# An eight-block transformer kernel on one core: row sums kept in PSUM, the last additions on VectorE, logits ahead of the row scales, and the output stored in four parts

## The chip, the cores and the metric

The kernel runs on one core of one Trainium2 chip. The metric is the device time of one execution in microseconds (us), as a median over runs. The profile shows one execution. Its engines are TensorE (PE, with its weight loads as PEld), VectorE (DVE), ScalarE (ACT), GpSimd (POOL) and SyncE (SP), which here only issues DMAs.

## The reference, cut to what matters

x is 4 batches of 512 rows of 256 numbers (float32). Eight blocks are added to it in turn; the change touches the two that are called `_L1_ffn_ref`, the sixth and the eighth.

```python
x = x + mla(_layernorm(x)); x = x + ffn(_layernorm(x)); x = x + cosine(_layernorm(x)); x = x + ffn(_layernorm(x))
x = x + gated_linear_attention(_layernorm(x))
x = x + _L1_ffn_ref(_layernorm(x), ...)      # stage wsa
x = x + lora_attention(_layernorm(x))
x = x + _L1_ffn_ref(_layernorm(x), ...)      # stage wsb
return x

def _L1_ffn_ref(x, workspace, ...):          # S = 16 slots, K = 4, NB = 2 rounds, 4 heads
    for _ in range(NB):
        logits = _rms(x, norm_pre_w) @ compete_w.T + compete_b
        vals, idx = top_k(swapaxes(logits, 1, 2), K)          # 4 rows of 512 for each slot
        written = softmax(vals)-weighted sum of the chosen rows of (x @ write_w.T + write_b)
        ws = _rms(ws + written, norm_post_w)
        att = softmax of (x @ wq.T + bq) against (ws @ wk.T + bk), over the 16 slots, 4 heads
        x_b = att applied to (ws @ wv.T + bv), @ out_proj_w.T + out_proj_b
        x = _rms(x + x_b, norm_post_w)
    return x
```

## The kernel before

The kernel is a row of stages. Each is one function with a block in which every engine runs its own hand-written list of instructions, held together by semaphores. After each stage `Kit.clear_sems` (L48 to L54) opens a block of its own in which POOL clears that stage's semaphores one by one; all engines meet at the start and at the end of each block. Nothing reorders the lists: what stands first in the code of an engine runs first.

`x` stays in SBUF for the whole program, as 16 tiles of 128 rows (4 for each batch). `workspace_ffn` runs twice, as stage `wsa` and, after `lora_attention`, as stage `wsb`. It works on `xf`, a normalised copy of x. At the start of a round PE turns the tiles of `xf` (`turn`, L1927) into two PSUM banks for each batch (`WS_TURN_BANKS`), ACT (round 0) or DVE (round 1) copies them out as `xfT`. Then:

- `spread_scales` (PE, L1937) puts the 16 columns of row scales `inv[:, 0, :]`, which POOL has computed (L1832), as rows into bank 4; it waits for the scales of batch 3 and for `xfT` of batch 1. ACT copies bank 4 to `rows` (L1888).
- `bid` (PE, L1947) multiplies `xfT` with the compete weights into bank 0: the logits. It waits for `xfT` of batch 3.
- `choose` (DVE, from L1692) waits for both, multiplies the logits by `rows`, and picks the four best rows. PE, DVE, ACT and POOL then hand the work to each other (`select`, `write`, `scores`, softmax, `read`) down to `read` (PE, L2040), which leaves the stage's x_b in the PSUM banks of each batch.
- `add_read(r, b)` (DVE, L1769) writes x_b + `xf` to `xsum`, an SBUF buffer for two batches; so it drains DVE before it uses a half again (batches 2 and 3).
- `mean_squares(1, b, ...)` (ACT, L1874) takes four squares with sums from `xsum`, `row_scales(1, b)` (POOL, L1830 and L1832) makes `inv[:, 1, :]` of them, and `norm_sum(r, b)` (DVE, L1778) writes the scaled rows to `xf`.

DVE's order at the end of a round is add 0, add 1, norm 0, add 2, norm 1, add 3, norm 2, norm 3. After round 1 POOL adds `xf` to `x`, one instruction of 128x1024 for each batch (L1862), and it does so after all of its row scales. After stage `wsb` and its clearing, `store_output` opens one more block, in which SP stores all of x with one DMA of 2 MB and waits for it (L2771).

## Time and profile before

| | us |
|---|---|
| median of 3 runs (2426.75 to 2430.74) | 2427.96 |
| the profiled execution, its own time | 2429.51 |
| span of the profiled execution, first to last instruction | 2427.7 |
| stage wsa, about | 1762 to 1911 |
| stage wsb, about | 2268 to 2416 |
| PE busy over the span | 2008.8 (83%) |
| DVE, ACT, POOL busy over the span | 1067.3, 801.7, 529.6 |

A busy share is an average over stages: in the two stages that the change touches PE is busy less than half of the time. Times in the rows below are us from the span's start. A row's bracket is the time for which the engine stood idle before it, and what ended that. PEclk is the granted clock of TensorE, 1.00 for 2.4 GHz and 0.50 for 1.2 GHz.

### The profile page before, as it was taken

To read this page: it belongs to the slowest core of one execution; us is meant where nothing else is said; L and a number is where in the kernel's file an instruction comes from. 1 tells how busy PE (TensorE), PEld (TensorE's weight loads), DVE (VectorE), ACT (ScalarE), POOL (GpSimd) and SP (SyncE) were. 2 spreads that over 40 slices of the span, in tenths; PEclk is the share of its full clock that TensorE was granted. 3 is DMA by queue.
4 is the path that set the end of the run, shared out by engine and by line. 5 is a ranking of instruction groups with operands and counts; after the bars stand their busy time and mean duration, and the time that the engine had idled before them with its cause. 6 is when DMAs were issued, how large, how long until landed. Compare 5 with 4: busy or idle time off the path is not lost. (4 is left out here: it accounts for less than half of the span.)

```text
span 2427.7 us, 28846 instructions
## 1 busy us (share of the span) xinstructions
PE 2008.8 (83%) x10760; PEld 1264.3 (52%) x10760; DVE 1067.3 (44%) x2279; ACT 801.7 (33%) x1749; POOL 529.6 (22%) x618
## 2 busy tenths in 40 slices
PE   7999999995799999999999994788755288889553
PEld 4565565654467766766666682333333144444332
DVE  4545545453223333332433223388555644445454
ACT  2544434451233233323323311411113134445132
POOL 2322323220101111011110000055311533342212
PEclk9999999997799999999999996999866689999666
DMA  6000000000000000000000001000000000000001
GB/s 239 1 1 1 1 1 1 1 1 30 1 1 1 1 1 1 1 1 1 1 1 1 1 1 63 0 0 0 0 1 1 1 1 1 1 1 1 1 1 35
DMA packets 9715, 23.87 MB, mean 10 GB/s; under 512 B 2400, under 2 KB 6256, under 8 KB 8816
## 3 DMA queue, kind: packets, MB, share of 16 engines
q1 hardware_dynamic: 8288, 18.92, 2.1%
q10 hardware_dynamic: 1296, 3.18, 0.4%
q8 instruction: 85, 1.39, 0.2%
q14 instruction: 46, 0.38, 0.1%
HBM read 20.00 MB, written 2.10 MB: 9 GB/s over the span
## 5 line engine op out<-in xcount | busy, mean ns | idle before, releaser
L1221 PEld LDWEIGHTS cos_ps<-cos_vx,cos_probs 128*128 128x128 f32 x2048 | 238.4, 191 | 33.6 <-issue 28.7
L1221 PE MATMUL cos_ps<-cos_vx,cos_probs 128*128 128x129 f32 x2048 | 239.5, 274 | 4.2 <-DVE cos_on L918 4.2
L1212 PE MATMUL cos_ps<-cos_qT,cos_kT 128*128 128x512 f32 x512 | 231.3, 596 | 1.4 <-ACT cos_qT L1074 1.4
L1103 ACT ACTIVATE cos_probs<-cos_ps 128x512 f32<-128x512 f32 x256 | 151.0, 598 | 161.9 <-PE cos_ps L1212 160.8
L366 ACT ACTIVATE probs<-sc,nmax 128x512 f32<-128x512 f32 (+3 forms) x256 | 132.6, 525 | 191.0 <-DVE nmax L229 189.0
L473 PE MATMUL sc<-kT,qT 128*128 128x512 f32 (+3 forms) x512 | 173.6, 461 | 4.3 <-DVE probsT L241 2.5
L1018 POOL TENSOR_TENSOR cos_qrs<-cos_qse,neg_half 128x4 f32<-128x4 f32 x64 | 64.5, 1008 | 511.2 <-DVE cos_qse L900 511.2
L2346 DVE TENSOR_REDUCE cos_wq<-lora_ps 128x2 f32<-128x1024 f32 (+3 forms) x128 | 101.9, 824 | 104.2 <-PE lora_ps L2589 103.2
L1212 PEld LDWEIGHTS cos_ps<-cos_qT,cos_kT 128*128 128x128 f32 x512 | 94.7, 192 | 97.4 <-issue 94.1
L898 DVE TENSOR_REDUCE cos_qss<-cos_qsq 128x4 f32<-128x512 f32 x64 | 43.9, 686 | 209.1 <-ACT cos_qsq L1082 209.1
L446 PE MATMUL pq<-xnT,wap 128*128 128x512 f32 x256 | 129.0, 628 | 3.1 <-DVE swp L221 3.1
L229 DVE TENSOR_REDUCE nmax<-sc 128x1 f32<-128x512 f32 (+3 forms) x256 | 112.5, 484 | 34.5 <-PE sc L475 31.7
L1200 PE MATMUL cos_ps<-cos_wq,cos_xnT 128*128 128x512 f32 x256 | 124.5, 610 | 0.0
L1241 PE MATMUL cos_ps<-cos_wout,cos_onT 128*128 128x256 f32 x512 | 115.7, 379 | 0.0
L2577 PE MATMUL lora_ps<-lora_kT,lora_qT 32*128 32x256 f32 (+3 forms) x512 | 103.8, 481 | 10.9 <-DVE lora_wvo L2324 2.7
L473 PEld LDWEIGHTS sc<-kT,qT 128*128 128x128 f32 x512 | 81.0, 193 | 60.6 <-issue 59.0
L1074 ACT ACTIVATE cos_qT<-cos_ps 128x512 f32<-128x512 f32 x64 | 38.2, 597 | 224.1 <-PE cos_ps L1191 224.1
L1426 POOL TENSOR_TENSOR gla_qs<-cos_wout,gla_q_now 128x512 f32<-128x512 f32 x64 | 84.8, 1324 | 113.5 <-DVE cos_wout L1380 110.2
L2464 ACT ACTIVATE lora_probsT<-lora_ps 128x768 f32<-128x768 f32 (+1 forms) x96 | 84.6, 882 | 61.9 <-PE lora_ps L2582 60.9
L2582 PE MATMUL lora_ps<-lora_qT,lora_kT 32*128 32x256 f32 (+3 forms) x512 | 102.5, 483 | 1.8 <-ACT lora_probsT L2464 1.1
L1241 PEld LDWEIGHTS cos_ps<-cos_wout,cos_onT 128*128 128x128 f32 x512 | 95.1, 190 | 13.3 <-issue 1.6
L2407 POOL TENSOR_SCALAR_AFFINE_SELECT lora_probsT<-lora_probsT 128x256 f32<-128x256 f32 x128 | 50.3, 410 | 204.0 <-ACT lora_probsT L2464 202.5
(462 smaller groups left out, 3503.0 us busy)
## 6 DMA issues: line engine op xcount, KB each, us to landing
onT<-in_mla_wqT SPq DMA_DIRECT2D x1, 2048.0 KB, 9.1
mla_wo<-in_mla_wo SPq DMA_DIRECT2D x1, 2048.0 KB, 19.4
cos_wq<-in_cos_wq SPq DMA_DIRECT2D x1, 2048.0 KB, 25.5
cos_wout<-in_cos_wout SPq DMA_DIRECT2D x1, 2048.0 KB, 29.9
out<-x SPq DMA_DIRECT2D x1, 2048.0 KB, 7.5
x<-in_x SPq DMA_DIRECT2D x1, 1536.0 KB, 14.6
wq_pe<-in_mla_wq_pe ACTq DMA_DIRECT2D x1, 1024.0 KB, 14.2
x<-in_x SPq DMA_DIRECT2D x1, 512.0 KB, 4.2
```

Of the source, the lines that this page charges most:

```text
L229: red = dve.tensor_reduce(nmax[:, j, qi:qi + 1], sc[:, j, at:at + (qi + 1) * P], AX.X, ALU.max, negate=True)
L366: ex = act.activation(probs[:, j, at:at + (qi + 1) * P], sc[:, j, at:at + (qi + 1) * P], ACT.Exp, bias=nmax[:, j, qi:qi + 1], accum_out=ls ...
L446: last = pe.matmul(pq[:, :], wap[:, c, p, kind, :], xnT[:, b % 2, c, :], start=(c == 0), stop=(c == DC - 1))
L473: pe.matmul(sc[:, j, at:at + (qi + 1) * P], qT[:, n % 2, j, qi * P:(qi + 1) * P], kT[:, b % 2, j, 0:(qi + 1) * P], start=True, stop=False)
L1103: act.activation(probs[:, n % 2, kj, :], ps[:, kj, :], ACT.Exp).then_inc(s["e_done"], 1)
L1200: last = pe.matmul(ps[:, banks["project", b, u], :], xnT[:, b % 2, c, i * P:(i + 1) * P], wq[:, c, 512 * hq:512 * (hq + 1)], start=(c == 0 ...
L1212: pe.matmul(ps[:, kj, :], kT[:, b % 2, kj * P:(kj + 1) * P], qT[:, hq % 2, h % 4, :], start=True, stop=True).then_inc(s["s_ready"], 1)
L1221: last = pe.matmul(po[:, qi // 2, qi % 2, :], probs[:, n % 2, kj, qi * P:(qi + 1) * P], vx[:, b % 2, kj, :], start=(kj == 0), stop=(kj == ...
L1241: last = pe.matmul(y[i], onT[:, n % 2, a, :], wout[:, 8 * half + a, :], start=(half == 0 and a == 0), stop=(half == 1 and a == 7))
L2346: last = dve.tensor_reduce(qs[:, batch % 2, qi, h:h + 2, LORA_HD], ps[:, at:at + 2, col:col + n], AX.X, ALU.max, negate=True)
L2577: pe.matmul(ps[:, at + j, col:col + w], qT[r:r + LORA_SLOT, qi * P:(qi + 1) * P], kT[r:r + LORA_SLOT, n % 2, 0:w], start=True, stop=False)
L2582: turned = pe.matmul(ps[:, at + 2 + j, col:col + w], kT[r:r + LORA_SLOT, t % 2, kj * P:(kj + 1) * P], qT2[r:r + LORA_SLOT, kj * P:], start ...
```

## The change

Both calls of `workspace_ffn`:

- `add_read` writes its sum back into the PSUM banks it reads; `xsum` is gone, and so is the drain for batches 2 and 3. ACT's squares and `norm_sum` read PSUM (`read_tile`).
- `norm_sum` of round 1 writes its product into PSUM too, drains, and adds it to `x` on DVE in two instructions of 128x512. POOL's four additions are gone.
- PE issues `bid` before `spread_scales`.

In stage `wsb` only: SP waits in the stage's own block for each batch of x and stores it with a DMA of 512 KB; the stage's block ends when all four have landed, and the clearing comes after that. `store_output` and its block are gone. Each stage has two semaphores more to clear, 52 for 50.

```diff
+            @block.sync
+            def _(sp):
+                if out is None:
+                    return
+                for b in range(B):
+                    sp.wait_ge(s["x_ready"], b + 1)
+                    sp.dma_start(out[b, :, :].rearrange("(i p) d -> p i d", p=P), x[:, tiles(b), :])\
+                      .then_inc(s["stored"], 16)
+                sp.wait_ge(s["stored"], 16 * B)
...
                     dve.wait_ge(s["xb_ready"], 2 * r + b // 2 + 1)
-                    if b >= 2:
-                        dve.drain()
                     for h in range(2):
                         at = b * TI + 2 * h
-                        last = dve.tensor_tensor(xsum[:, b % 2, 2 * h:2 * h + 2, :],
-                                                 bank(read_bank(b, h)).rearrange("p (i d) -> p i d", i=2),
-                                                 xf[:, at:at + 2, :], ALU.add)
+                        both = bank(read_bank(b, h)).rearrange("p (i d) -> p i d", i=2)
+                        last = dve.tensor_tensor(both, both, xf[:, at:at + 2, :], ALU.add)
...
-                        last = dve.scalar_tensor_tensor(xf[:, n, :], xsum[:, b % 2, i, :], inv[:, 1, n:n + 1],
+                        rows_out = xf[:, n, :] if r + 1 < WS_NB else read_tile(b, i)
+                        last = dve.scalar_tensor_tensor(rows_out, read_tile(b, i), inv[:, 1, n:n + 1],
                                                         g["ws_post"][:, :], ALU.mult, ALU.mult)
-                    last.then_inc(s["xf_ready"], 1)
+                    if r + 1 < WS_NB:
+                        last.then_inc(s["xf_ready"], 1)
+                        return
+                    dve.drain()
+                    for h in range(2):
+                        at = b * TI + 2 * h
+                        last = dve.tensor_tensor(x[:, at:at + 2, :],
+                                                 bank(read_bank(b, h)).rearrange("p (i d) -> p i d", i=2),
+                                                 x[:, at:at + 2, :], ALU.add)
+                    last.then_inc(s["x_ready"], 1)
...
-                for b in range(B):
-                    pool.wait_ge(s["xf_ready"], WS_NB * B + b + 1)
-                    pool.tensor_tensor(x[:, tiles(b), :], xf[:, tiles(b), :], x[:, tiles(b), :], ALU.add)
...
-                        mean_squares(1, b, [xsum[:, b % 2, i, :] for i in range(TI)]).then_inc(s["m2_ready"], 1)
+                        mean_squares(1, b, [read_tile(b, i) for i in range(TI)]).then_inc(s["m2_ready"], 1)
...
+                    bid(r)
                     spread_scales(r)
-                    bid(r)
```

On DVE at the end of stage `wsb` (round 1) the list of before is, from `add_read` of batches 0 and 1 on (line numbers are those of each kernel; `wsb_ps` is PSUM):

```order
L1769 TENSOR_TENSOR wsb_xsum<-wsb_ps,wsb_xf 128x512 x4
L1778 SCALAR_TENSOR_TENSOR wsb_xf<-wsb_xsum,wsb_inv,ws_post 128x256 x4
L1769 TENSOR_TENSOR wsb_xsum<-wsb_ps,wsb_xf 128x512 x2
L1778 SCALAR_TENSOR_TENSOR wsb_xf<-wsb_xsum,wsb_inv,ws_post 128x256 x4
L1769 TENSOR_TENSOR wsb_xsum<-wsb_ps,wsb_xf 128x512 x2
L1778 SCALAR_TENSOR_TENSOR wsb_xf<-wsb_xsum,wsb_inv,ws_post 128x256 x8
```

and after it:

```order
L1780 TENSOR_TENSOR wsb_ps<-wsb_ps,wsb_xf 128x512 x4
L1788 SCALAR_TENSOR_TENSOR wsb_ps<-wsb_ps,wsb_inv,ws_post 128x256 x4
L1796 TENSOR_TENSOR x<-wsb_ps,x 128x512 x2
L1780 TENSOR_TENSOR wsb_ps<-wsb_ps,wsb_xf 128x512 x2
L1788 SCALAR_TENSOR_TENSOR wsb_ps<-wsb_ps,wsb_inv,ws_post 128x256 x4
L1796 TENSOR_TENSOR x<-wsb_ps,x 128x512 x2
L1780 TENSOR_TENSOR wsb_ps<-wsb_ps,wsb_xf 128x512 x2
L1788 SCALAR_TENSOR_TENSOR wsb_ps<-wsb_ps,wsb_inv,ws_post 128x256 x4
L1796 TENSOR_TENSOR x<-wsb_ps,x 128x512 x2
L1788 SCALAR_TENSOR_TENSOR wsb_ps<-wsb_ps,wsb_inv,ws_post 128x256 x4
L1796 TENSOR_TENSOR x<-wsb_ps,x 128x512 x2
```

The two additions to x of batches 0, 1 and 2 stand ahead of the next batch's work on the same engine; those of batch 3 are the last.

At the very end, POOL before (the `ISA` rows are the clearing of semaphores):

```order
L1832 TENSOR_TENSOR wsb_inv<-wsb_mse,neg_half 128x4
L1862 TENSOR_TENSOR x<-wsb_xf,x 128x1024 x4
L1665 UNCONDITIONAL_BRANCH
L51 UNCONDITIONAL_BRANCH
L54 ISA x50
L50 UNCONDITIONAL_BRANCH
```

and POOL after:

```order
L1851 TENSOR_TENSOR wsb_inv<-wsb_mse,neg_half 128x4
L1667 UNCONDITIONAL_BRANCH
L51 UNCONDITIONAL_BRANCH
L54 ISA x52
L50 UNCONDITIONAL_BRANCH
```

The additions have left POOL, and the DMAs, which stood behind the clearing, now stand ahead of it (on SP, `L1674 DMA out<-x 128x4x256 x4`).

On PE at the head of a round the rows of before and, below them, those of after:

```order
L1927 MATMUL wsb_ps<-ident,wsb_xf 128x128 x32
L1937 MATMUL wsb_ps<-ident,wsb_inv 32x128 x16
L1947 MATMUL wsb_ps<-wsb_xfT,wsb_cw 32x512 x8
L1954 MATMUL wsb_ps<-ident,wsb_selw 128x128 x4
```

```order
L1943 MATMUL wsb_ps<-ident,wsb_xf 128x128 x32
L1963 MATMUL wsb_ps<-wsb_xfT,wsb_cw 32x512 x8
L1953 MATMUL wsb_ps<-ident,wsb_inv 32x128 x16
L1970 MATMUL wsb_ps<-ident,wsb_selw 128x128 x4
```

The logits (`wsb_cw`) and the row scales (`wsb_inv`) have changed places; this holds in both rounds of both stages. ACT's copy of the spread scales, which DVE waits for, so comes behind both.

## Rows read from the trace of the kernel before

**Rows 1.** The page, its first part: busy us, share of the span, instructions.

```profile
PE 2008.8 (83%) x10760; PEld 1264.3 (52%) x10760; DVE 1067.3 (44%) x2279; ACT 801.7 (33%) x1749; POOL 529.6 (22%) x618
```

**Rows 2.** Timeline (start us, us, what) of DVE, stage wsb, end of round 1.

```profile
2395.97 1.68 DVE L1778 SCALAR_TENSOR_TENSOR wsb_xf<-wsb_xsum,wsb_inv,ws_post 128x256 f32<-128x256 f32 x4 [2.19 <-POOL wsb_inv L1832]
2397.74 1.29 DVE L1769 TENSOR_TENSOR wsb_xsum<-wsb_ps,wsb_xf 128x512 f32<-128x512 f32 x2
...
2400.70 1.29 DVE L1769 TENSOR_TENSOR wsb_xsum<-wsb_ps,wsb_xf 128x512 f32<-128x512 f32 x2
...
2405.38 7.93 DVE L1778 SCALAR_TENSOR_TENSOR wsb_xf<-wsb_xsum,wsb_inv,ws_post 128x256 f32<-128x256 f32 x4 [1.30 <-POOL wsb_inv L1832]
```

**Rows 3.** Timeline of POOL, the same stretch.

```profile
2404.33 1.01 POOL L1832 TENSOR_TENSOR wsb_inv<-wsb_mse,neg_half 128x4 f32<-128x4 f32 x1
2405.50 7.52 POOL L1862 TENSOR_TENSOR x<-wsb_xf,x 128x1024 f32<-128x1024 f32 x3 [0.16 <-issue]
2413.38 2.34 POOL L1862 TENSOR_TENSOR x<-wsb_xf,x 128x1024 f32<-128x1024 f32 x1 [0.36 <-DVE wsb_xf L1778]
```

**Rows 4.** Timeline, end of stage wsa (POOL) and start of the next stage (DVE).

```profile
1908.48 2.35 POOL L1862 TENSOR_TENSOR x<-wsa_xf,x 128x1024 f32<-128x1024 f32 x1 [0.36 <-DVE wsa_xf L1778]
1914.95 1.41 DVE L61 BATCH_NORM_STATS2 lora_stats<-x 128x6 f32<-128x256 f32 x4 [6.55 <-PEq L50]
```

**Rows 5.** Timeline of DVE, start of stage wsa.

```profile
1761.90 1.41 DVE L61 BATCH_NORM_STATS2 wsa_stats<-x 128x6 f32<-128x256 f32 x4 [2.81 <-PEq L50]
```

**Rows 6.** Timeline of SP: the issue of the output's DMA.

```profile
2419.81 0.40 SPq L2771 DMA_DIRECT2D out<-x  x1
```

**Rows 7.** The page, DMA issues: KB each, us from issue to landing.

```profile
out<-x SPq DMA_DIRECT2D x1, 2048.0 KB, 7.5
...
x<-in_x SPq DMA_DIRECT2D x1, 512.0 KB, 4.2
```

**Rows 8.** Windows: stretch, us, busy us (count) by engine, PEclk, DMA share, GB/s.

```profile
2422.00:2423.00 1.00, 0.00 (x0) 0.00 (x0) 0.00 (x0) 0.00 (x0) 0.00 (x0) 0.50 1.03 345
```

**Rows 9.** Timeline of ACT, DVE and PE, stage wsb, head of round 0.

```profile
2285.24 1.09 ACT L1869 ACTIVATE wsb_xfT<-wsb_ps 128x512 f32<-128x512 f32 x2 [0.62 <-PE wsb_ps L1927]
2286.64 0.60 ACT L1888 ACTIVATE wsb_rows<-wsb_ps 128x512 f32<-128x512 f32 x1 [0.31 <-PE wsb_ps L1937]
...
2288.45 0.69 DVE L1692 TENSOR_TENSOR wsb_lraw<-wsb_ps,wsb_rows 128x512 f32<-128x512 f32 x1 [4.22 <-PE wsb_ps L1947]
...
2281.53 3.67 PE L1927 MATMUL wsb_ps<-ident,wsb_xf 128*128 128x128 f32 x16 [2.00 <-DVE wsb_xf L1675]
```

**Rows 10.** Timeline of DVE, stage wsb, head of round 1.

```profile
2342.29 4.88 DVE L1686 COPY wsb_xfT<-wsb_ps 128x512 f32<-128x512 f32 x8
2353.58 0.69 DVE L1692 TENSOR_TENSOR wsb_lraw<-wsb_ps,wsb_rows 128x512 f32<-128x512 f32 x1 [6.41 <-PE wsb_ps L1947]
```

**Rows 11.** Windows: wsb, L1937 and L1947 of round 0, L1937 of round 1, two turns.

```profile
2285.49:2286.47 0.98, 0.98 (x33) 0.84 (x34) 0.00 (x0) 0.83 (x2) 0.00 (x0) 1.00 0.00 0
2286.47:2288.39 1.92, 1.92 (x20) 0.46 (x16) 0.00 (x0) 0.60 (x1) 0.00 (x0) 1.00 0.04 9
2348.40:2350.11 1.71, 1.71 (x33) 1.58 (x36) 0.00 (x0) 0.00 (x0) 0.00 (x0) 0.50 0.00 0
2339.38:2344.28 4.90, 3.87 (x16) 3.10 (x16) 3.66 (x8) 4.54 (x21) 3.60 (x5) 0.50 0.00 2
```

**Rows 12.** Windows: stage wsa, L1947 of round 1.

```profile
1844.42:1848.06 3.64, 3.64 (x23) 0.59 (x12) 0.00 (x0) 0.60 (x1) 0.00 (x0) 0.51 0.00 0
```

**Rows 13.** Groups by line and shape: out<-in xcount, busy us, mean ns, idle before.

```profile
L1376 DVE TENSOR_TENSOR gla_ps<-gla_ps,gla_kT 128x512 f32<-128x512 f32 x64 | 43.4, 678 | 4.6 <-ACT gla_decay L1458 3.2 <-PE gla_ps L1522 1.4
L1720 DVE TENSOR_TENSOR wsb_wsum<-wsb_ps,wsb_wsb 128x256 f32<-128x256 f32 x2 | 0.9, 426 | 2.4 <-PE wsb_ps L1971 2.4
L1797 DVE TENSOR_TENSOR wsb_wsb<-ws_start,ws_write_b 128x256 f32<-128x256 f32 x1 | 0.4, 420 | 0.0
L1913 ACT ACTIVATE wsb_ash<-wsb_ash 128x512 f32<-128x512 f32 x4 | 2.5, 630 | 4.2 <-DVE wsb_ash L1750 4.2
```

More of the change, by code:

```diff
@@ L1594, with workspace_ffn @@
 WS_TURN_BANKS = ((0, 2), (4, 6), (1, 3), (5, 7))
-def workspace_ffn(nc, g, tag):
+def workspace_ffn(nc, g, tag, out=None):
     with ExitStack() as ctx:
@@ L1610, in workspace_ffn @@
         xf = sb("xf", [P, NT, D])
-        xsum = sb("xsum", [P, 2, TI, D])
         xfT = sb("xfT", [P, DC, NT * P])
@@ L1651, in workspace_ffn @@
                  "a_ready", "a_copied", "at_ready", "ash_ready", "ae_ready", "att_ready", "pt_ready", "attT_ready",
-                 "xb_ready", "xsum_ready", "m2_ready", "r2_ready")
+                 "xb_ready", "xsum_ready", "m2_ready", "r2_ready", "x_ready", "stored")
         s = {n: k.sem(f"{tag}_{n}") for n in names}
@@ L1663, in read_bank, with read_tile @@
             return WS_TURN_BANKS[b][half]
+        def read_tile(b, i):
+            return bank(read_bank(b, i // 2))[:, (i % 2) * D:(i % 2 + 1) * D]
         with nc.Block() as block:
+            @block.sync
[7 more added lines that the diff above has]
+                sp.wait_ge(s["stored"], 16 * B)
             @block.vector
@@ L2756, in build @@
         lora_attention(nc, g)
-        workspace_ffn(nc, g, "wsb")
-        store_output(nc, g, out)
-def store_output(nc, g, out):
-    with ExitStack() as ctx:
-        stored = Kit(nc, ctx).sem("stored")
-        with nc.Block() as block:
-            @block.sync
-            def _(sp):
-                sp.dma_start(out.rearrange("b (i p) d -> p (b i) d", p=P), g["x"][:, :, :]).then_inc(stored, 16)
-                sp.wait_ge(stored, 16)
+        workspace_ffn(nc, g, "wsb", out)
 def kernel(**inputs):
```

## The prediction

> **What bounds the kernel now.** Read first the page's busy shares: PE 83% [rows 1]. That would make every edit off PE worthless, and it is an average. So the next view is the timeline of the two stages that change, wsa and wsb, and there the idle times in the brackets: at each step one engine waits for another, and no engine is the bound. What counts is the chain of handovers. Three places of it matter.
>
> The end of a stage. At 2405.34 POOL has the last row scales (2404.33 + 1.01) [rows 3]; from then on only DVE's last `norm_sum` and the four additions to x are left. DVE's takes 7.93 us where the same four instructions took 1.68 three batches earlier [rows 2]. Beside them POOL runs three additions in 7.52 us, and the fourth, 2.34, after DVE [rows 3]. The two engines hold each other up. The stage's work ends at 2413.38 + 2.34 = 2415.72.
>
> The end of the program. From 2415.72 to the DMA's issue at 2419.81 [rows 6] there are 4.09 us in which POOL clears 50 semaphores and the engines meet; the DMA lands 7.5 us later [rows 7], at 2427.3, and the span ends at 2427.7.
>
> The head of a round. DVE waits for `bid` (L1947), 4.22 us in round 0 [rows 9] and 6.41 in round 1 [rows 10]. `spread_scales` runs ahead of it, and ACT's copy of the scales (0.60) lies beside `bid` [rows 9].
>
> **Part 1: additions on DVE.** Walk through round 1 of wsb from 2395.97 [rows 2]. I use: four products 1.67, two sums 1.29, 0.09 for a drain (2397.65 to 2397.74), and an instruction that doesn't wait starts 0.08 before the end of the one ahead. Norm 0 ends at 2397.65, its new additions run 2397.74 to 2399.03, add 2 ends at 2400.24, norm 1 at 2401.83, its additions at 2403.2, add 3 at 2404.41 (before: 2400.70 + 1.29 = 2401.99), norm 2 with its additions at 2407.4. The scales of batch 3 came 3.35 after add 3 (2405.34 - 2401.99), so now at 2407.76: DVE has been free for 0.4. Norm 3 and its drain and additions take 1.67 + 0.09 + 1.29: x is complete at 2410.85, and 2415.72 - 2410.85 = **4.9 us** are gained. In wsa the stage's last addition ends at 1908.48 + 2.35 = 1910.83 [rows 4], with the same distances, so **4.9 us** again. These additions were not free on POOL; on DVE, 2.4 of their 5.2 us delay add 3, and that is in the walk.
>
> **Part 2: sums in place in PSUM.** DVE's sum: 128x512 in place in PSUM took 678 ns in another stage [rows 13], against 0.69 for such an operation with its output in SBUF [rows 9]: nothing. DVE's product with PSUM on one or both sides is not in the trace. Nearest: an addition of 128x256 with one input in PSUM 426 ns, with both in SBUF 420 [rows 13]. I take 0, bounds -0.02 and +0.07 for each. Some 12 products are on the chain of a round, 48 in all: -1.0 to +3.4 us. A rule speaks against this: the Trainium skill ("VectorE: DVE Perf Modes", The TRN2 errata) gives a VectorE operation 58 cycles over its elements from SBUF and 120 from PSUM, which would be an estimate of 65 ns more for each product, or 3.1 us over the 48. The trace's 426 against 420 disagrees with it, so the sum goes without.
>
> ACT's squares read PSUM. A 128x512 pass took 0.60 from PSUM [rows 9] and 630 ns from SBUF, with another function [rows 13]; so -0.03 each, eight on the chain of a round, 32 in all: -1.0, bounds -1.5 and 0. I take half, **-0.5**.
>
> The drain ahead of add 2 and add 3: without it the sum starts 0.08 before the product's end instead of 0.09 behind it, 0.17 each. Both feed the chain to the scales of batch 3 in round 0: 4 x 0.17 = **-0.7**. In round 1 the walk has it.
>
> **Part 3: logits first.** Round 0 of wsb: `xfT` of batch 3 is there at 2286.33 (2285.24 + 1.09) [rows 9], `bid` started at 2286.47, so it gains 0.1. Then 0.98 of `spread_scales` [rows 11], which lay in PE's idle time, stands behind `bid`, and behind it ACT's copy with its handovers, 0.7, which lay beside `bid`: DVE starts at 2286.4 + 1.92 + 0.98 + 0.7 = 2290.0 for 2288.45, **+1.6**. That is with the clock at 1.00. Before the change it rose while PE went from the turns into `spread_scales` with at most 0.3 of idle time; now there is a pause of 1.2 us between the last turn (2281.53 + 3.67 = 2285.20 [rows 9]) and `bid`. In round 1 two turns with a pause of 1.0 between them stayed at 0.50 to their end [rows 11]. At 0.50 `bid` takes 3.64 and `spread_scales` 1.71 [rows 11, 12], so the head would take 1.7 + 0.7 more: **+4.0**. When the clock rises differs from run to run, and was in this execution already up for both; I take +2.3 for the mix (bounds 1.6 and 4.0).
>
> Beside that the Trainium skill ("TensorE: Matmul & The Clock Gate", Part 1) says that the gate's observation runs free of the kernel, so that the place where the clock rises shifts from run to run. The trace is one run and shows one place.
>
> Round 1 of wsb: the copies end at 2342.29 + 4.88 = 2347.17 [rows 10], the scales only at about 2348.4 [rows 11]. `bid` (3.64) ends at 2350.8, `spread_scales` (1.71) at 2352.5, less some 0.3 for a clock that rises on the way, the copy at 2352.9: DVE starts 0.6 ahead of 2353.58, **-0.6**. wsa is alike: its heads hold the same rows. For two stages: 2 x (2.3 - 0.6) = **+3.4**, bounds +2.0 and +6.8.
>
> **Part 4: the output.** Three of the four DMAs are issued from 2399.0, 2403.2 and 2407.4 and are done before the last. That one moves 512 KB. 2 MB took 7.5; at the 345 GB/s of its middle [rows 8] 1.5 MB are 4.6 us, so 2.9 are left; the 512 KB load at the program's start took 4.2 [rows 7]. I take 3.4. Nothing is queued behind SP's waits but the four DMAs. The 4.09 of meeting and clearing come after the landing now, with two more semaphores: the 32 semaphores of the stage ahead of wsa took 2.81 (the bracket of the first instruction of wsa) [rows 5], 50 took 4.12 (1910.83 to 1914.95) [rows 4], so 0.07 each and 0.15 for two. Before: 4.09 + 7.5 + 0.4 = 12.0 from the last addition to the span's end; now 3.4 + 4.1 + 0.15 + 0.1 = 7.75, **-4.2** (-4.7 to -3.4). The clearing moved, it did not go. wsa clears two more as well: **+0.15**.
>
> **The sum.** -4.9 - 4.9 - 0.5 - 0.7 + 3.4 - 4.2 + 0.15 = -11.65 against the profiled 2429.51, so 2417.9. The profiled execution stands 1.55 above the median of 2427.96; against that, **2416.3**.
>
> **Rivals.**
> 1. The clock doesn't rise in round 0. For: the pause of 1.2, and the turns at 0.50 across a pause of 1.0. Against: later stretches that began cold do rise. All four heads cold and late: +6.8 instead of +3.4, so 2419.7.
> 2. The last DMA's time hardly depends on its size (7.5 for 512 KB also). Against: the 4.2 row. It gives back 4.1: 2420.4.
> 3. The new products cost more with PSUM (0.07 each, 3.4 in all), by the skill's rule named above nearly the same. 2419.7.
> 4. The clearing at the very end isn't part of the measured time, since nothing waits for it. For: no row shows an execution that ends with one. Against: the program isn't over. 2412.2.
> 5. Slower than before: DVE and ACT, both in PSUM now at the end of each round, hold each other up as DVE and POOL did. The chain has 48 products, so it decides from 11.65 / 48 = 0.24 us on each; at a contention of 1.0 each (DVE beside POOL lost 7.93 - 1.67 = 6.3 on four) the time would be 2416.3 + 48 = 2464. Against: the in-place sums in PSUM at 678 ns ran with ACT at work there.
> 6. That the output isn't stored early: x's last batch is late anyway, so only the size of the last DMA counts. That is rival 2's price.
>
> **How the numbers follow.** Forecast 0.52, rival 1 0.20, rivals 2 and 6 0.07, rival 3 0.09, rival 4 0.08, rival 5 0.04. The range from 2411.5 to 2421.0 takes in all but the last and the sum of two bad cases. This kernel's measurement can tell 0.2%, 4.9 us: faster means below 2423.1. Faster 0.93, same 0.04, slower 0.03.
>
> **What would show it.** DVE's last `norm_sum` back at 1.7 us with the additions right behind it, and 4.9 us less from the first add of a last round to the end of the stage's work. `spread_scales` and the copy on the way from `bid` to DVE; PEclk over `bid` in round 0. The last output DMA 3 to 4 us, then some 4 us of clearing. Products near 480 ns. It is wrong if the products or squares in PSUM come out longer, if the span ends with the landing, or if the heads of round 0 cost over 4 each.

## The result, and the profile after

The changed kernel takes 2420.80 us as a median of 8 runs (2419.21 to 2423.56), the kernel before beside it 2427.43 (8 runs, 2425.68 to 2430.74). The ratio is 0.9972, with a 95% interval of 0.9961 to 0.9982: 6.6 us faster, between 4.4 and 9.5. The forecast was 11.65 us less, 2416.3. Direction and range held, the range by 0.2 us (its upper end is 2421.0); a little over half of the gain came. The measured time of an execution is 1.8 us longer than its span, before and after.

The profiled execution of the changed kernel has a span of 2421.8 us, against 2427.7, so 5.9 less. It is cut below at the same places in both. "Head" is from the start of a stage (round 0) or of the copies of `xfT` (round 1) to the product of the logits with `rows`; "choice" from there to the sum that takes the written slots; "attention" from there to the first `add_read`; "end" from there to the next round's copies, or to the last addition to x; "behind it" to the next stage or to the end of the span.

| us | before | after | difference |
|---|---|---|---|
| the three stages ahead of wsa | 1761.9 | 1762.6 | +0.7 |
| head, round 0: wsa, wsb | 20.20, 20.26 | 23.19, 21.77 | +3.0, +1.5 |
| head, round 1 | 11.53, 11.29 | 10.18, 10.26 | -1.35, -1.0 |
| choice, round 0 | 13.18, 12.99 | 14.24, 14.23 | +1.1, +1.2 |
| choice, round 1 | 13.00, 13.04 | 14.24, 14.54 | +1.2, +1.5 |
| attention, four rounds | 100.4 | 101.3 | +0.8 |
| end, round 0 | 15.84, 15.84 | 15.16, 15.16 | -0.7, -0.7 |
| end, round 1 | 24.44, 24.42 | 19.18, 19.20 | -5.3, -5.2 |
| behind wsa, behind wsb | 4.12, 11.98 | 4.31, 7.28 | +0.2, -4.7 |
| lora_attention, which nothing touches | 353.2 | 355.0 | +1.8 |

The end of the stages came as walked through. This is the timeline of DVE in stage wsb, end of round 1, of the changed kernel (start us, us, what; the bracket is idle time before, and what ended it):

```profile
2395.32 2.49 DVE L1780 TENSOR_TENSOR wsb_ps<-wsb_ps,wsb_xf 128x512 f32<-128x512 f32 x4 [4.60 <-PE wsb_ps L2056]
2399.88 1.67 DVE L1788 SCALAR_TENSOR_TENSOR wsb_ps<-wsb_ps,wsb_inv,ws_post 128x256 f32<-128x256 f32 x4 [2.06 <-POOL wsb_inv L1851]
2401.62 1.29 DVE L1796 TENSOR_TENSOR x<-wsb_ps,x 128x512 f32<-128x512 f32 x2
...
2409.89 1.29 DVE L1796 TENSOR_TENSOR x<-wsb_ps,x 128x512 f32<-128x512 f32 x2
2411.49 1.67 DVE L1788 SCALAR_TENSOR_TENSOR wsb_ps<-wsb_ps,wsb_inv,ws_post 128x256 f32<-128x256 f32 x4 [0.32 <-POOL wsb_inv L1851]
2413.23 1.29 DVE L1796 TENSOR_TENSOR x<-wsb_ps,x 128x512 f32<-128x512 f32 x2
```

The last product takes 1.67 us where it took 7.93 [rows 2], it waits 0.32 for its scales (forecast 0.4), and x is complete 1.3 us after it. The products with PSUM on both sides cost what they cost from SBUF.

SP's timeline and the page's DMA issues (KB each, us from issue to landing) show the output, and the page's clock line its lower places (tenths of full speed in 40 slices):

```profile
2402.94 11.98 SPq L1674 DMA_DIRECT2D out<-x  x4
```

```profile
out<-x SPq DMA_DIRECT2D x4, 512.0 KB, 2.9
```

```profile
PEclk9999999998799999999999997999866689999666
```

Four stores of 512 KB land 2.9 us after their issue, where the one of 2 MB took 7.5 [rows 7]. The three sixes in the middle lie over stage wsa, the last three over wsb: there the clock is low for most of the time. The kernel before has the same six sixes on its page. The timeline of PE, stage wsa, round 0, from the logits to the written slots, first of the kernel before, then of the changed one:

```profile
1778.83 1.47 PE L1937 MATMUL wsa_ps<-ident,wsa_inv 128*32 128x128 f32 x32
1780.13 1.89 PE L1947 MATMUL wsa_ps<-wsa_xfT,wsa_cw 128*32 128x512 f32 x16
1786.87 1.12 PE L1954 MATMUL wsa_ps<-ident,wsa_selw 128*128 128x128 f32 x4 [4.85 <-DVE wsa_selw L1706]
1788.77 3.64 PE L1959 MATMUL wsa_ps<-wsa_xf,wsa_selT 128*32 128x256 f32 x32 [0.78 <-DVE wsa_selT L1709]
1793.02 0.57 PE L1965 MATMUL wsa_ps<-ident,wsa_xsel 128*128 128x128 f32 x2 [0.61 <-DVE wsa_xsel L1711]
1794.11 1.13 PE L1971 MATMUL wsa_ps<-ws_write,wsa_xselT 128*128 128x256 f32 x4 [0.52 <-DVE wsa_xselT L1713]
```

```profile
1780.70 3.44 PE L1963 MATMUL wsa_ps<-wsa_xfT,wsa_cw 128*32 128x512 f32 x16 [1.27 <-ACT wsa_xfT L1885]
1783.96 1.06 PE L1953 MATMUL wsa_ps<-ident,wsa_inv 128*32 128x128 f32 x32
1790.56 1.11 PE L1970 MATMUL wsa_ps<-ident,wsa_selw 128*128 128x128 f32 x4 [5.54 <-DVE wsa_selw L1718]
1792.46 3.64 PE L1975 MATMUL wsa_ps<-wsa_xf,wsa_selT 128*32 128x256 f32 x32 [0.78 <-DVE wsa_selT L1721]
1796.71 0.69 PE L1981 MATMUL wsa_ps<-ident,wsa_xsel 128*128 128x128 f32 x2 [0.61 <-DVE wsa_xsel L1723]
1797.92 2.08 PE L1987 MATMUL wsa_ps<-ws_write,wsa_xselT 128*128 128x256 f32 x4 [0.52 <-DVE wsa_xselT L1725]
```

Two things are to be seen. The first: with the logits first, `bid` waits 1.27 us for the copies, the pause that the prediction named, and takes 3.44 us for 1.89. In stage wsb of the same execution the same pause stands ahead of `bid`, and `bid` has the high clock (the rows of before for this place are [rows 9], which are of wsb though their heading says wsa):

```profile
2287.09 1.92 PE L1963 MATMUL wsb_ps<-wsb_xfT,wsb_cw 128*32 128x512 f32 x16 [1.27 <-ACT wsb_xfT L1885]
```

So the pause alone doesn't settle which clock `bid` gets. The second: behind the choice the four matmuls that write the slots take 2.08 us for 1.13, and the two before them 0.69 for 0.57: that is the 1.06 us of the choice, at the same waits between the engines from there on. The windows of the changed kernel (stretch, us, busy us and count by engine, PEclk, DMA share, GB/s) give the clock of `bid`, of `spread_scales`, and of the stretch from the choice on:

```profile
1780.70:1784.14 3.44, 3.44 (x24) 1.06 (x28) 0.00 (x0) 0.00 (x0) 0.00 (x0) 0.55 0.00 0
1783.96:1785.02 1.06, 1.06 (x36) 0.79 (x28) 0.00 (x0) 0.00 (x0) 0.00 (x0) 1.00 0.00 0
1790.56:1803.50 12.94, 8.21 (x44) 3.85 (x44) 2.76 (x7) 0.51 (x2) 1.47 (x3) 0.50 0.01 2
```

`bid` runs almost wholly at 1.2 GHz (0.55), the clock rises at its end, `spread_scales` has 2.4 GHz (1.00), PE stands idle for 5.54 us while DVE chooses, and all that follows has 1.2 GHz again (0.50).

### The profile page after: what moved, and what is told of

The parts are those of the page before. It is cut to its first block and busy times, and to the rows that moved or that the text cites. A ratio compares the mean times of both kernels' runs of the same rounds, so it can differ in the third digit from the quotient of the medians.

```text
span 2421.8 us, 28850 instructions
## 1 busy us (share of the span) xinstructions
PE 2018.0 (83%) x10760; PEld 1271.6 (53%) x10760; DVE 1063.2 (44%) x2295; ACT 798.9 (33%) x1749; POOL 508.3 (21%) x610
## 5 line engine op out<-in xcount | busy, mean ns | idle before, releaser
L241 DVE COPY probsT<-sc 128x512 f32<-128x512 f32 (+1 forms) x128 | 65.4, 553 | 65.0 <-PE sc L487 65.0
## 6 DMA issues: line engine op xcount, KB each, us to landing
x<-in_x SPq DMA_DIRECT2D x1, 1536.0 KB, 14.4
```

## The experiments

Three questions: which part of the change gives what; is the loss behind the heads the clock's, and does it come from PE's pauses; and where does lora_attention's time come from. Each median stands against that of the kernel before on the same chip, with the difference in us.

**The order undone.**

```diff
-                    bid(r)
                     spread_scales(r)
+                    bid(r)
                     select(r)
```

> The changed kernel with spread_scales ahead of bid again, in both rounds of both stages; all else as changed. My theory: the order of the heads costs time, 3.4 us by the prediction, and the two traces put +3.0 and +1.5 on the heads of round 0 against -1.35 and -1.0 on those of round 1; so 2.1 to 5 us faster than the changed kernel, about 2417 (7 to 8 us at most if the colder clock behind the heads, +1.1 to +1.5 in each stretch from choose to the written slots, is a consequence of the order too: 2413). Rival A: the order is free on the average over executions and the shortfall sits in PSUM operands or the stores: 2420 to 2421.

Measured: 2417.10 us (2411.29 to 2418.04, 5 runs), ratio 0.9954 [0.9941, 0.9967], -9.3 us. Without the swap the kernel is 2.7 us better placed against before than with it, as the theory had it, though the intervals of the two ratios still overlap (the changed kernel's begins at 0.9961). In the profile the heads of round 0 are back at 20.21 and 20.19, and the choice takes 13.18, 13.83, 13.04 and 13.24, 4.0 less in all. All stretches of wsa and wsb together are 7.1 us shorter than in the changed kernel; lora_attention took 358.8 us in that execution, 3.8 more. The heads of round 1 took 10.19 in wsa, as with the logits first, and 11.53 in wsb.

**The order alone**, the same two lines in the kernel before.

> The kernel before with bid ahead of spread_scales and nothing else. My theory: +2 to +5 us, about 2431; with the colder clock behind the heads as a consequence up to +7. Rival A: 2427 to 2428, no change.

Measured: 2435.24 us (2431.32 to 2440.59, 6 runs), ratio 1.0038 [1.0026, 1.0050], +8.8 us: the swap alone makes the kernel slower than it was, by more than the 7 us that the theory gave at most. In the profile it is +3.0 and +1.6 in the heads of round 0, -0.4 and -1.4 in those of round 1, +1.05 and +1.25 in the choice of round 0, +0.03 and +0.44 in that of round 1, and +0.8 in the attention: 6.4 us in the two stages, where the prediction had 3.4. (The span of that execution is only 2.0 longer, since the three stages ahead took 4.4 less in it.)

**The additions alone**, in the kernel before: DVE adds `xf` to x, POOL's four instructions are gone.

```diff
+                    dve.drain()
+                    for h in range(2):
+                        at = b * TI + 2 * h
+                        dve.tensor_tensor(x[:, at:at + 2, :], xf[:, at:at + 2, :], x[:, at:at + 2, :], ALU.add)
...
-                    pool.tensor_tensor(x[:, tiles(b), :], xf[:, tiles(b), :], x[:, tiles(b), :], ALU.add)
```

> The kernel before with the additions to x on VectorE (from xf, behind a drain, in two instructions for each batch) in place of GpSimd's four, nothing else changed. My theory: 4.9 us less at the end of each stage, 9.8 in all: 2417.6. Rival: the additions moved ahead of the next batches' sums on VectorE take back more than the walk says: 2420 or above.

Measured: 2420.72 us (2417.45 to 2426.32, 11 runs), ratio 0.9973 [0.9964, 0.9982], -5.7 us. The ends of round 1 take 20.28 and 20.29 us for 24.44 and 24.42, so -4.15 each, where 4.9 was expected; the median misses its forecast of 2417.6 and lies where the rival had it, at 2420 or above. The walk left out two things: this kernel keeps the two drains (0.34 by the prediction's 0.17 each), and its last row scales come 3.8 us after the sum of batch 3, for 3.35. The median moved less than the two ends (8.3); the rest isn't explained. This one edit has nearly the median of the whole change (-5.7 and -6.6). The end on DVE, in its timeline:

```profile
2402.16 1.67 DVE L1778 SCALAR_TENSOR_TENSOR wsb_xf<-wsb_xsum,wsb_inv,ws_post 128x256 f32<-128x256 f32 x4 [0.90 <-POOL wsb_inv L1838]
2403.91 1.29 DVE L1786 TENSOR_TENSOR x<-wsb_xf,x 128x512 f32<-128x512 f32 x2
```

Nothing of POOL stands beside it, and the products from SBUF take 1.67 us for four, as those from PSUM do.

**The sums in SBUF again**, all else as changed.

```diff
-                        last = dve.tensor_tensor(both, both, xf[:, at:at + 2, :], ALU.add)
+                        last = dve.tensor_tensor(xsum[:, b % 2, 2 * h:2 * h + 2, :],
+                                                 bank(read_bank(b, h)).rearrange("p (i d) -> p i d", i=2),
+                                                 xf[:, at:at + 2, :], ALU.add)
```

> The changed kernel with the row sums in SBUF again (xsum, the drain for batches 2 and 3, squares and products reading SBUF, the product of the last round written to xf and added to x from there); logits first, additions on VectorE and the four stores stay. My theory: keeping the sums in PSUM gains; the traces show the end of round 0 0.68 us shorter in each stage and the last end about 0.3, so this kernel is 1.5 to 2.5 us slower than the changed one, about 2422.5. Rival B: products or squares on PSUM cost time somewhere: 2 us faster, about 2418.5.

Measured: 2421.11 us (2416.07 to 2425.78, 5 runs), ratio 0.9967 [0.9954, 0.9980], -5.3 us. The ends take 15.82, 20.32, 15.82 and 20.30 us, so the sums in place are worth 0.66 in a round 0 and 1.1 in a round 1, 3.6 in all. The whole kernel's median doesn't show them (the changed one has -6.6): the choice of round 1 takes 13.03 and 13.48 here, 2.3 less than in the changed kernel, where the shorter ends stand ahead of a longer choice. They are the 13.03 and 13.48 of `e3`, which has the same order and SBUF sums too. The profile is 2.1 us longer; by the medians the two can't be told apart.

**A filler in the pause ahead of `bid`** (round 0).

```diff
+                    if r == 0:
+                        pe.wait_ge(s["xfT_ready"], 2)
+                        for i in range(4):
+                            pe.transpose(bank(4)[:, 0:P], ident[:, :], ident[:, :])
                     bid(r)
```

> The changed kernel with four transposes of the identity on TensorE in the pause of 1.2 us between the last turn and bid, round 0 of both stages. If that pause is what keeps the clock down, the head of wsa's round 0 goes from 23.2 to about 21.7 us, bid from 3.4 to 1.9, and wsb's stays at 21.8; the kernel is 1 to 2 us faster, about 2419. If the clock rises at a place of its own there, both heads stay as they are, and nothing changes.

Measured: 2419.77 us (2416.54 to 2421.0, 5 runs), ratio 0.9963 [0.9950, 0.9976], -8.3 us. The timeline of PE in wsa:

```profile
1777.19 1.06 PE L2069 MATMUL wsa_ps<-ident 128*128 128x128 f32 x4
1778.66 1.92 PE L1963 MATMUL wsa_ps<-wsa_xfT,wsa_cw 128*32 128x512 f32 x16 [0.41 <-ACT wsa_xfT L1885]
```

The pause is 0.41 for 1.27 us and `bid` 1.92 for 3.44; the head of wsa takes 21.67 for 23.19, as much as wsb's, whose `bid` had the high clock already (1.92). So work in the pause brought the high clock forward to `bid` in wsa; in wsb of the changed kernel `bid` had it across the whole pause. The median moved by no more than can be told.

**A short filler during the choice.**

```diff
                 def select(r):
+                    for i in range(22):
+                        pe.transpose(bank(1)[:, 0:P], ident[:, :], ident[:, :])
                     pe.wait_ge(s["selw_ready"], r + 1)
```

> The changed kernel with 22 transposes of the identity into a free PSUM bank on TensorE while it waits for VectorE's choice of rows, in all four rounds. If the stretches from the logits' use to the written slots (14.2 to 14.5 us in the changed kernel's profile, 13.0 to 13.2 in that of before) are longer because the granted clock stays at 0.50 there, they go to 13.0 or below in all four, and the kernel gets 4 to 8 us faster, 2414 to 2417. If they are longer for another reason (a handover, PSUM operands), they stay at 14.2 and the fillers cost up to 0.5 each.

Measured: 2421.62 us (2418.17 to 2424.21, 9 runs), ratio 0.9973 [0.9963, 0.9983], -6.4 us. The choice takes 14.20, 14.12, 13.89 and 14.54 us, 0.5 less in all: next to nothing. In the timeline of PE the filler ran 2.62 us at the high clock, and then PE stood idle again:

```profile
1780.74 2.62 PE L1969 MATMUL wsa_ps<-ident 128*128 128x128 f32 x22
1786.36 1.07 PE L1975 MATMUL wsa_ps<-ident,wsa_selw 128*128 128x128 f32 x4 [2.99 <-DVE wsa_selw L1718]
1788.21 3.64 PE L1980 MATMUL wsa_ps<-wsa_xf,wsa_selT 128*32 128x256 f32 x32 [0.78 <-DVE wsa_selT L1721]
```

By this run alone the theory of the pauses would have fallen. But it left 3 us of pause, so it had not taken the supposed cause away.

**The filler up to the choice's end**, 44 for 22.

> The changed kernel; PE does 44 transposes of the identity into the free bank 1 while VectorE chooses the rows, where e6_filler_in_choose had 22 of them and then stood idle for 3.0 us. At the 0.119 us each of that run they fill 5.2 of the 5.6 us in front of the choice, so the pause is 0.4. Their results aren't read. Theory (the stretch from the logits to the written slots is longer since the clock is down over its matmuls, and it is down because PE pauses in front of them): the 32 matmuls that gather the chosen rows take 1.9 us instead of 3.64, the 4 that write 1.13 instead of 2.08, and the stretch takes 11.5 to 12.5 us instead of 14.2 in each of the four rounds; the stages are shorter by 7 to 10 us in all, lora_attention gives back 0 to 5 of it, 2413 to 2418 us. Rival (the clock's place there doesn't come from the pause in front of the choice): the stretch stays at 13.9 to 14.5 in at least two rounds, 2420 to 2422.

Measured: 2405.96 us (2404.63 to 2413.3, 5 runs), ratio 0.9913 [0.9898, 0.9929], -22.4 us. The same place of PE's timeline:

```profile
1779.63 5.02 PE L1969 MATMUL wsa_ps<-ident 128*128 128x128 f32 x44
1785.24 0.66 PE L1975 MATMUL wsa_ps<-ident,wsa_selw 128*128 128x128 f32 x4 [0.59 <-DVE wsa_selw L1718]
1786.68 1.93 PE L1980 MATMUL wsa_ps<-wsa_xf,wsa_selT 128*32 128x256 f32 x32 [0.78 <-DVE wsa_selT L1721]
1789.23 0.44 PE L1986 MATMUL wsa_ps<-ident,wsa_xsel 128*128 128x128 f32 x2 [0.61 <-DVE wsa_xsel L1723]
1790.18 1.13 PE L1992 MATMUL wsa_ps<-ws_write,wsa_xselT 128*128 128x256 f32 x4 [0.52 <-DVE wsa_xselT L1725]
```

With a pause of 0.6 us instead of 5.5 every matmul behind it has the high clock: 0.66 for 1.11, 1.93 for 3.64, 0.44 for 0.69, 1.13 for 2.08. The choice takes 10.88, 10.87, 10.88 and 11.18 us, below the 13.0 to 13.2 of the kernel before, where the gather of the rows took 3.64 too, behind a pause of 4.85. It is 13.4 us less than in the changed kernel; lora_attention stayed at 355.0, and the median went down by 15.8. The rival falls, and the gain is larger than the forecast (7 to 10 us in the stages, 2413 to 2418): it had the choice at 11.5 to 12.5. The long filler differs from the short one in two things at once, less pause and more work of PE; 22 transposes put right ahead of the end of the wait, which would tell them apart, were not run.

The Trainium skill ("TensorE: Matmul & The Clock Gate", "Why this matters for your kernels") says that pauses of PE between bursts put the clock back; the two fillers agree, 10.88 us against 14.20, with nothing different but the count of transposes. Its Part 1 says that the place of the change differs between runs of one kernel, and two profiles here bear it out: `e1` above and `e5` below have the same code up to the end of wsa's work, and their choice in wsa's round 0 took 13.18 and 14.24 us. The last four matmuls of it, in `e1` and in `e5`:

```profile
1792.48 1.13 PE L1987 MATMUL wsa_ps<-ws_write,wsa_xselT 128*128 128x256 f32 x4 [0.52 <-DVE wsa_xselT L1725]
```

```profile
1795.65 2.08 PE L1991 MATMUL wsa_ps<-ws_write,wsa_xselT 128*128 128x256 f32 x4 [0.52 <-DVE wsa_xselT L1725]
```

Both have a pause of 4.85 us ahead of the choice. With the row scales first and no filler (`before`, `e1`, `e4`, `e5`, `e7`, `e9`) the choice of round 0 took 12.99 to 13.20 us in 11 of 12 cases and 14.24 in this one; with the logits first (the changed kernel, `e2`, `e3`, `e11`) it took 14.23 or 14.24 in all eight. So the order goes with the longer choice, but by what step isn't shown: it makes the pause longer, 5.54 for 4.85, yet wsa in `e8` had 5.54 too and a choice of 12.87.

**The order by round**: row scales first in round 0, where the logits lose the clock, logits first in round 1, where they gain.

```diff
+                    if r == 0:
+                        spread_scales(r)
                     bid(r)
-                    spread_scales(r)
+                    if r > 0:
+                        spread_scales(r)
```

> The changed kernel with spread_scales first in round 0 and bid first in round 1. By the profiles the heads of round 0 go back to 20.2 us (from 23.2 and 21.8) and those of round 1 stay at 10.2 (11.3 to 11.5 with the scales first). My theory: as e1 or 1 us faster, 2416 to 2417, unless the clock's place in later stages moves it. Rival A (order is free): 2420 to 2421.

Measured: 2414.51 us (2411.49 to 2415.61, 5 runs), ratio 0.9941 [0.9928, 0.9953], -13.5 us. Heads of 20.21, 10.35, 20.20 and 10.11 us, with lora_attention at 358.5. That is 1.5 us under the forecast and 6.9 better placed than the changed kernel. Against the order undone in both rounds (`e1`, -9.3) it is not clear: the intervals overlap, and in the profiles the heads of round 1 give 1.3 (20.5 for 21.7), of which the choice and the attention take back 1.0, so that the two stages together differ by 0.2 us.

**lora_attention.** The first question was whether its time follows from the time at which it starts.

```diff
                     dve.drain()
+                if out is None:
+                    for n in (S, S, S, D):
+                        dve.tensor_scalar(lt[:, 0:n], lraw[:, 0:n], g["ws_cb"][:, 0:1], None, ALU.add)
+                        dve.drain()
```

At the end of stage wsa, first on the kernel with the order undone, then on the changed kernel:

> The kernel of e1_scales_first with about 2.1 us of useless work on VectorE at the end of stage wsa (three passes of 128x512 and one of 128x256 over a scratch tile), which every engine waits for. Stage lora_attention, whose code no kernel here touches, took 353.2 to 353.9 us in the profiles of the kernel before, e3 and e4, but 355.0 in the changed kernel, 357.1 in e2 and 358.7 in e1. My theory: it depends on where the stage begins relative to the changes of TensorE's granted clock, which go on upstream of it in the same way in every kernel; this wait moves its start back to a place equivalent to that of the kernel before, so lora_attention takes 353 to 354.5 us in the profile and the whole is 2 to 4 us faster than e1 in spite of the added wait (2413 to 2415). Rival C: lora's time varies by chance from run to run: it may be anything from 353 to 359, and the kernel is on the median 2 us slower than e1 (2419).

> The changed kernel, with about 2.1 us of work on VectorE, whose results aren't read, at the very end of stage wsa. lora_attention, which no edit touches, took 353.3 us in the kernel before, 355.0 in the changed kernel, where it starts 1.8 us sooner after the same work, and 358.4 to 358.7 in three kernels where it starts 5.1 to 5.5 sooner. Theory (the time of lora_attention follows from when it starts against what PE did ahead of it, and repeats): with its start moved back by 2.1 it takes 353 to 354.5 us, the other stretches of the changed kernel stay within 0.1, and the median comes to 2420.3 to 2422. Rival (its 1.7 to 5.4 us are chance of single executions): 355 to 358.7, 2422 to 2424.

Measured: 2416.83 us (2411.4 to 2423.96, 6 runs), ratio 0.9953 [0.9937, 0.9969], -11.2 us for the first; 2427.46 us (2424.93 to 2430.31, 11 runs), ratio 0.9995 [0.9986, 1.0004], -0.9 us for the second. The stretch behind wsa is 2.1 us longer in both. lora_attention took 356.1 us in the first, 2.6 less than without the wait, where 353 to 354.5 was expected, and 359.7 in the second, 4.7 more, where the same was expected. The theory falls in its form, that the start alone sets it. The rival, pure chance, had 2422 to 2424 for the second and misses it too: all its 11 runs lie above all 8 of the changed kernel, and against the kernel before it lost 5.7 us for 2.1 us of work. Chance is not out of it for the single profiles: the kernel before alone ran from 2425.2 to 2431.0 in 15 executions beside the second, and the stages ahead of wsa, the same code in every kernel, differ by up to 6.1 us between profiles.

What the profiles do show is where in lora_attention the time goes. The first 16 matmuls with the weights `wqk` in PE's timeline, of the kernel before, of the changed one and of the second wait:

```profile
1928.20 7.13 PE L2502 MATMUL lora_ps<-lora_wqk,lora_xnT 128*128 128x512 f32 x16 [1.33 <-DVE lora_wqk L2324]
```

```profile
1927.41 8.70 PE L2518 MATMUL lora_ps<-lora_wqk,lora_xnT 128*128 128x512 f32 x16 [1.32 <-DVE lora_wqk L2340]
```

```profile
1928.64 9.33 PE L2522 MATMUL lora_ps<-lora_wqk,lora_xnT 128*128 128x512 f32 x16 [1.32 <-DVE lora_wqk L2344]
```

The windows of the first 17 us of the stage, before and after, give the clock:

```profile
1914.95:1931.95 17.00, 7.44 (x25) 4.57 (x26) 10.85 (x29) 1.80 (x4) 8.77 (x8) 0.66 0.00 1
```

```profile
1913.90:1930.90 17.00, 7.47 (x21) 4.36 (x22) 10.83 (x29) 1.20 (x2) 7.73 (x7) 0.51 0.00 1
```

The same 16 matmuls take 1.6 us more in the changed kernel, whose lora_attention is 1.8 longer, and 2.2 more in the one with the wait, whose lora_attention is 6.5 longer. There a longer stretch at the low clock comes on top; the windows from 51 to 55 us after the stage's start, of the changed kernel and of the one with the wait:

```profile
1964.90:1968.90 4.00, 4.00 (x16) 1.51 (x15) 0.27 (x1) 1.09 (x2) 0.00 (x0) 1.00 0.02 4
```

```profile
1966.10:1970.10 4.00, 3.67 (x7) 1.65 (x6) 1.37 (x2) 0.00 (x0) 0.00 (x0) 0.50 0.00 0
```

16 matmuls ran in four microseconds in the one, 7 in the other. In the kernel with the order by round, whose lora_attention took 358.5 us, a second difference is to be seen. DVE's timeline of that kernel, and that of the next one below (`e9_clearing_beside_last_store`, 355.2 us), which does the same work up to there:

```profile
1908.44 7.24 DVE L2330 TENSOR_SCALAR lora_xn<-x,lora_mv,lora_rstd 128x256 f32<-128x256 f32 x4
```

```profile
1911.34 4.78 DVE L2329 TENSOR_SCALAR lora_xn<-x,lora_mv,lora_rstd 128x256 f32<-128x256 f32 x4
```

The same four instructions, with POOL's memsets beside them in both, took 7.24 us in the one and 4.78 in the other, and the 16 matmuls began 2.46 us later after the stage's start. What decides between the two, and what puts the clock's rise earlier or later for the same work, stays open.

**The clearing beside the last store**, with the order by round.

```diff
                     sp.dma_start(out[b, :, :].rearrange("(i p) d -> p i d", p=P), x[:, tiles(b), :])\
-                      .then_inc(s["stored"], 16)
-                sp.wait_ge(s["stored"], 16 * B)
+                      .then_inc(g["stored"], 16)
...
         workspace_ffn(nc, g, "wsb", out)
+        with nc.Block() as block:
+            @block.sync
+            def _(sp):
+                sp.wait_ge(g["stored"], 16 * B)
```

> The changed kernel with the order of PE by round (row scales first in round 0, logits first in round 1, as in e7_order_by_round) and another end: stage wsb doesn't wait for its four stores; the semaphores are cleared while the last one is under way, and a block of its own after that waits for all four on a semaphore that is not among the cleared ones. In e7_order_by_round 7.25 us lie between the last addition to x and the end of the span, in a row: the store with its handover 2.9, then meeting and clearing 4.1 to 4.3. Theory (the two don't need one another, and the clearing is in the measured time): only the longer of the two is left, with one more meeting of the engines of 0.1 to 0.5, so 4.3 to 4.8 between the last addition and the end, 2.5 to 2.9 less, and 2411.8 us against 2414.5. Rival (GpSimd's clearing and a DMA under way hold each other up, or the additional block costs as much as is hidden): 2413 to 2415.

Measured: 2413.93 us (2409.32 to 2414.25, 5 runs), ratio 0.9934 [0.9921, 0.9948], -14.4 us. From the last addition to the end of the span it is 4.99 us, for 7.25: 2.3 less, a little under the forecast of 2.5 to 2.9. The median lies where the rival had it (2413 to 2415), and 0.9 better placed than without the edit, so the end by itself can't be told by the medians: the 2.3 us rest on the two profiles.

**All of it**: this kernel with the filler of the choice (38 transposes in round 0, 44 in round 1).

> The kernel of e9_clearing_beside_last_store (order of PE by round, clearing beside the last store) with the transposes of e10_filler_up_to_select in front of the choice: 38 in round 0, where PE stood idle for 4.83 to 4.85 us there, and 44 in round 1, where it was 5.5 to 5.9. At 0.114 us each they leave 0.5 us of pause. Theory (the three terms lie in different stretches and so add up): the heads of round 0 take 20.2 us, the stretch from the logits to the written slots 10.9 in all four rounds, for 13.2, 14.2, 13.05 and 13.55, so 10.4 us less in the stages, and 5.0 us from the last addition to the end; with lora_attention between 353 and 359 the span comes to 2397 to 2403, the median to 2399 to 2405. Rival (lora_attention and the rest of the stages give back what is taken out, since their matmuls meet the clock elsewhere): 2406 to 2411.

Measured: 2402.97 us (2401.55 to 2403.62, 4 runs), ratio 0.9903 [0.9886, 0.9919], -23.7 us. Heads of round 0 20.21 and 20.17, choices 10.88, 10.88, 10.89 and 11.19, 5.03 behind the last addition, lora_attention 355.0. The terms lie where they were expected, and this is the kernel with the lowest median, 17.1 us better placed than the changed one. The filler alone (-22.4) gives most of that: the two intervals overlap.

## Why the prediction was right or wrong

**Part 1, right.** -4.9 for each stage were forecast, -5.3 and -5.2 measured with the sums in place, a little more than the walk's, and -4.15 with this edit alone (`e4`). POOL and DVE did hold each other up.

**Part 2, right.** Products 0: four took 1.67 us before and after. By the estimate that the prediction drew from the Trainium skill ("VectorE: DVE Perf Modes", The TRN2 errata) the 48 products would have cost 3.1 us; the trace decides against it once more, and rival 3 falls with it. ACT's squares took 0.38 us for 0.41. The ends of round 0 gave 0.7 each, of which 0.35 was the drains' by the forecast. With part 1 the forecast is -11.0, the profile -11.8.

**Part 4, right, and a little better.** The last store took 2.9 for 3.4, the output -4.7 for -4.2; rivals 2 and 6 fall. The two more semaphores cost 0.19 in wsa for 0.15. Rival 4 falls: 7.3 us of store and clearing lie inside the span, the measured time is the span and 1.8 us with the clearing at its end as it was without, and hiding the one behind the other in `e9` shortened the span.

**Rival 5** falls. DVE's four products took 1.66 us in PSUM while ACT's squares ran in PSUM beside them, and 1.67 without. The Trainium skill ("SBUF — State Buffer", "SBUF: two separate sides") says that among the engines only VectorE and GpSimd wait on each other in SBUF. POOL's additions before agree with it, 7.93 for 1.68; of PSUM that section says nothing.

**Part 3 was wrong, not in the head but behind it.** For the heads +3.4 was forecast and +2.1 measured: +3.0 in the one of round 0 that lost the clock, +1.5 in the one that kept it, where +4.0 and +1.6 were worked out, and -1.35 and -1.0 in round 1 for -0.6. "wsa is alike" was not so: the two heads of round 0 differ by 1.4 us. The step that failed is that the swap's price ends with the head. The prediction looked at the clock over the two matmul groups that it swaps, and left what stands behind them at the durations of the trace before. But the choice follows, in which PE stands idle, and with the order turned round the clock is down over more of the small matmuls behind it: +5.0 us over the four rounds, 4.0 of which go when the order is undone (`e1`), and +0.8 in the attention. Not all of it is the order's alone: with the order and without the sums in PSUM it is +2.8 in the four choices (`e3`, `e2`), so 2.3 us, all in round 1, came with the shorter ends ahead of it, or differ by execution (`e11`, with the changed kernel's code in wsb, has 13.30 there for 14.54); no run tells the two apart. These 5.9 us, the 1.8 of lora_attention, and 0.7 that the three stages ahead differed by, turn the -14.2 of the terms that had a price into the -5.9 of the spans, rounding aside. Rival 1 had the mechanism, a clock that doesn't rise, and a price for the heads alone.

**The range held by luck.** The terms with a price came out 2.6 us better than forecast (-14.2 for -11.65), the whole median 0.2 under the range's end. With the same loss behind the heads and the terms as forecast, the time would have lain above it.

That the clock makes the choice long is shown by its matmuls, twice the time at the same waits, and that PE's idle time ahead of it puts the clock down by the filler that closes the pause and takes 3.4 us out of each round, where the one that leaves 3 us of it takes out next to nothing. Why the clock rises again later with the logits first is not shown. For lora_attention it is shown that its matmuls meet the low clock for longer, and not why.

**The order may belong to the round.** A gain of 0.6 in round 1 and a loss of 2.3 in round 0 stood in the prediction side by side. That is a case for turning round the order in round 1 only, which `e7` did, for -13.5 us against the -6.6 of the change as it was made. What is shown is that round 0 wants its row scales first; whether logits first in round 1 gain anything over `e1` (-9.3) is not.

## What to carry to other kernels

When an edit moves matmuls against a pause of TensorE, price everything up to the next long stretch of work at both clocks, not only what is moved, and expect that time gained at one place changes the clock at the next. A pause that waits for another engine can be filled with transposes whose result nobody reads, but only if they last up to the end of the wait: half a filler was worth next to nothing here, a whole one 3.4 us each time. Two edits with opposite signs in two rounds of the same loop are two edits, and are to be tried apart. And where the clock changes inside a chain of small matmuls, one profile of each kernel isn't enough: the same code gave 13.18 and 14.24 us in two of them.

## What the runs showed of the hardware

- TensorE's work that nobody needs was the largest gain of the study: 44 transposes in each of four pauses, 13.4 us in the stages.
- The choice of wsa's round 0 took the same time to 0.1 us in kernels that differed elsewhere (14.23, 14.24, 14.20), low clock included, but 13.18 and 14.24 in two kernels with the same code up to there (`e1`, `e5`). The three untouched stages ahead together took 1757.3 to 1763.3 us.
- A product of 128x256 with input and output in PSUM took 483 ns, from PSUM to SBUF 476, and an addition of 128x512 690 in PSUM in place.
- Clearing 52 semaphores, with the meetings, takes 4.3 us, and can lie beside a DMA's landing.
- Work of 2.1 us between two stages cost 5.7 us in the changed kernel (-0.9 against -6.6, each from the kernel before beside it), and nothing that could be told in the one with the other order (-11.2 against -9.3, overlapping intervals).
